# Attention over 16 rows, then a triangle product: reordering the first and last steps of the attention loop

## The chip, the cores and the metric

The kernel runs on one core of a Trainium2 chip. Its five engines each run their own instruction stream and meet at semaphores: TensorE (PE), VectorE (DVE), ScalarE (ACT), GpSimd (POOL) and SyncE (SP), which here only issues DMAs. The metric is the device time of one launch in microseconds (us).

## The reference

Two residual layers on x of shape (16, 32, 32, 32). The change touches the first layer, and the preparation of the second layer's weights and biases. Cut to what matters:

```python
x = x + attention(gn(x))            # layer one, gn: group norm over rows and columns
# attention, for every (a, b) position and 8 heads of 16 channels, over the 16 rows n:
zn = layernorm(z) * ln_w + ln_b
q, k, v = zn @ Wq, zn @ Wk, zn @ Wv
g = sigmoid(zn @ Wg + bg)
att = softmax(einsum('iabhc,jabhc->ijabh', q, k) / 4, axis=1)
out = (einsum('ijabh,jabhc->iabhc', att, v) * g) @ Wo + bo
x = x + triangle(gn(x))             # layer two
# triangle: a, b = sigmoid(zn @ W_g + b_g) * (zn @ W_l + b_l), two pairs of weights
# k = einsum('bitc,bjtc->bijc', a, b); sigmoid(zn @ W_go + b_go) * (norm(k) @ W_lo + b_lo)
```

## The kernel before

Every engine's order is written out by hand; there is no scheduler. The first layer is a software pipeline over eight blocks of four columns b (NS = 8, a block is 128 x 512 values). Period j works on three blocks at once: block j from its layer norm to its score exponentials, block j-1 from the softmax sum to the transposed probabilities ("tail"), block j-2 from the product with z to the gated output and the residual ("B"). Periods 0 to 2 stand in front of a loop of four, written periods 3 to 6; periods 7, 8 (NS) and 9 (NS + 1) stand behind it. Periods 8 and 9 have no block j of their own, and period 9 has no tail.

What one period holds, in the names of the code and of the profile:

- TensorE: `pe_u` (products of the transposed probabilities PT with Z, to `u_sb`), `pe_znT` (transposes of `zn_tok`), `pe_t` (znT with A_bd, eight heads, in three banks, so head h waits for the low part of head h-3), `pe_o` (u_sb with Wv_p), `pe_PT` (four transposes of P), `pe_scores` (t_sb with zbd, four groups), `pe_gate`, `pe_out` (og with Wo_h).
- float32 values go to TensorE as a high and a low float16 part. For t: ACT casts the high part (L628), DVE subtracts the low part (L936). For the probabilities P, which lie in `S_sb` as float32: ACT casts P's high part into `PP` (`p_high`, L622), and `p_low` (L444) subtracts; in period 1 DVE does that, in all later periods POOL. For the normalised block: ACT casts `zn_tok` (`act_ln_high`, L588), POOL subtracts its low part (`pool_ln_low`, L431).
- DVE also takes the scores' maximum (`nmax`, L953) and subtracts it (L957), sums the exponentials (L868) and inverts the sums (`rden`, L887), gates the output (`gate_o`, `og`, L907), copies two of four transposed groups of P (`PT_copy`, L912; ACT has the other two, L644), adds the residual (`dve_x1`, L897) and reduces x1 and its square for the second group norm (`dve_stats`, L873, and `dve_stats_sq`, L879).
- ACT also makes the exponentials (`exps`, L634), the gates' tanh (`gates`, L639) and the copies of u (L614).
- POOL: the layer norm's power (`pool_ln_rstd`, L418), the normalisation of P by `rden` (`pool_norm`, L438), the layer norm's scale and shift (`pool_ln_scale`, L423 to L427), `pool_sqx` (x1 squared, L451), `pool_ln_low`, and the group-normed block j+3 (`pool_ln_front`, L410 to L414).

`dve_weights2` splits the second layer's weights into high and low parts: 28 small instructions on 32 partitions (L977 to L989). `dve_biases2` splits its biases in three: 6 small instructions (L995 to L1004). POOL then spreads the three bias parts into `B1` (L554) and clears two buffers of 128 x 4096 float32 (L549: `x_tok`, L558: `PP`). TensorE takes the first product of the second layer's statistics (`g2_mm`) only when all of that preparation has been counted (`wprep2`), and when DVE has summed the statistics of all eight blocks.

Of the kernel before, what the change touches and what calls it, by code (L numbers as in the profile page):

```python
# [28 lines left out]
NS = L // SB  # L29
# [7 lines left out]
def build(nc, x, ln_w, ln_b, Wq, Wk, Wv, Wg, bg, Wo, bo, al_in, be_in, W_la, b_la, W_ga, b_ga,  # L37
          W_lb, b_lb, W_gb, b_gb, al_o, be_o, W_go, b_go, W_lo, b_lo, out):
    ctx = ExitStack()
    with ctx:  # L40
# [392 lines left out]
        def pool_norm(pool, m, ks):  # L433

            pool.wait_ge(p_rec, 2 * m + ks[0] // 2 + 1)
            for k in ks:
                P = S_sb[:, 8 * k:8 * k + 8].rearrange("p q a n -> p (q a) n")
                nc.gpsimd.tensor_tensor(P, P, bcast(rden[:, 32 * k:32 * k + 32], 2, N), ALU.mult).then_inc(p_nrm, 1)  # L438
# [13 lines left out]

        def pool_period(pool, j, par, tail=True, stats=True):
            LN = j + 1 < NS
            own = tail and not (j == 1)
            if LN:
                pool_ln_rstd(pool, j + 1, 1 - par)
            if tail:
                pool_norm(pool, j - 1, (0, 1))
                pool_norm(pool, j - 1, (2, 3))  # L460
            if LN:
                pool_ln_scale(pool, j + 1, 1 - par)
            if own:
                p_low(pool, nc.gpsimd, j - 1, (0, 1))
            if stats:
                pool_sqx(pool, j - 3)
            if own:
                p_low(pool, nc.gpsimd, j - 1, (2, 3))
            if LN:
                pool_ln_low(pool, j + 1, 1 - par)  # L470
            if j + 3 < NS:
                pool_ln_front(pool, j + 3, 1 - par)
# [134 lines left out]
        def act_period(act, j, par, half, tail=True, B=True, A=True, LN=True):  # L607
# [34 lines left out]
            def PT_copy(k):  # L642
                act.wait_ge(pt_mm, 4 * m + k + 1)
                nc.scalar.copy(PT[:, 8 * k:8 * k + 8].rearrange("p q m -> p (q m)"),  # L644
                               bank_b(k)[:, :].bitcast(f16)).then_inc(pt_ok[1], 1)
# [7 lines left out]
            if early:  # L653

                if j == 0:
                    t_high(range(5))
                    act_ln_square(act, 2, 0)
                    t_high(range(5, H))
                    act_ln_high(act, 1, 1, 0)
                    nc.scalar.activation(scrap[:, 0:1], minus_half[:, 0:1], ACT.Tanh)  # L660
                    act_weights(act)
                else:
                    t_high((0, 1, 2))
                    p_high((0, 1))
                    t_high((3, 4))
                    p_high((2, 3))
                    act_ln_square(act, 3, 1)
                    t_high((5, 6, 7))
                    PT_copy(1)
                exps((0,))  # L670
                gates((0, 1))
                exps((1,))
                if j == 1:
                    PT_copy(3)
                gates((2, 3))
                if j == 0:
                    act_znT(act, 1)
                else:
                    act_ln_high(act, 2, 0, 1)
                exps((2, 3))  # L680
                return
            if A:
# [217 lines left out]
        def dve_period(dve, j, par, tail=True, B=True, A=True, stats=True):  # L900
# [23 lines left out]
                dve_ln_centre(dve, j + 2, par)  # L924
            if stats:
                dve_stats(dve, s - 1)
            if j == NS:
                dve_weights2(dve)
            if j == NS + 1:
                dve_biases2(dve)  # L930

            for h in range(H if A else 0):
                if h == 3 and B:
                    gate_o(range(A2))
                dve.wait_ge(t_hi, H * j + h + 1)
                nc.vector.tensor_tensor(t_sb[:, LO, :, h], bank_tg(h)[:, :].rearrange("p (q i) -> p q i", i=N),  # L936
                                        t_sb[:, HI, :, h], ALU.subtract).then_inc(t_lo, 1)
                if j == 0 and h == 0:
                    dve_gate_weights(dve)
                if j == 0 and h == 2:  # L940
                    dve_ln_centre(dve, 2, 0)
                if j == 1 and h in (2, 4):
                    p_low(dve, nc.vector, 0, (h - 2, h - 1))
            if B and not A:
                gate_o(range(A2))
            if tail:
# [3 lines left out]
            for k in range(4 if A else 0):  # L950
                S = bank_s(k)[:, :].rearrange("p (r n) -> p r n", n=N)
                dve.wait_ge(s_mm, 4 * j + k + 1)
                nc.vector.tensor_reduce(nmax[:, k % 2], S, op=ALU.max, axis=AX.X).then_inc(s_max, 1)  # L953
                if tail:
                    dve.wait_ge(p_lo, 4 * m + k + 1)
                dve.wait_ge(s_max, 4 * j + k + 1)
                nc.vector.tensor_tensor(S_sb[:, 8 * k:8 * k + 8].rearrange("p q a n -> p (q a) n"), S,  # L957
                                        bcast(nmax[:, k % 2], 2, N), ALU.subtract).then_inc(s_sub, 1)
                if k == 1 and stats:
                    dve_stats_sq(dve, s - 1)  # L960
                if k == 2 and tail:
                    PT_copy(2)
            if stats and not A:
                dve_stats_sq(dve, s - 1)
            if tail and not A:
                PT_copy(2)

        WP1 = 3 + 4 + 1 + 1

# [581 lines left out]
```

## Time and profile before

| what | us |
|---|---|
| median of 3 runs (lowest, highest) | 329.82 (329.68, 332.94) |
| the profiled execution: its time | 330.46 |
| its span in the trace | 328.4 |
| busy in the span: PE, DVE, ACT, POOL | 245.6, 256.8, 214.8, 196.9 |
| share of the chain that ended last: DVE, PE, ACT, issue, POOL | 43%, 35%, 7%, 5%, 5% |
| mean granted clock of TensorE (share of full) | 0.907 |

Rows of the timeline have the start, the duration, the engine, the line of kernel.py, the instruction, what it writes and reads, and in brackets the idle time in front of it with the instruction that ended it. A row with x2 to x64 is a run of like instructions. Rows of the chain have start, duration and what stood on the path that ended last.

### The profile page before, as it was taken

Reading aid. Unit: us, or ns where it says so; the run is one execution under the profiler, and the core shown is the slowest. Engines: PE = TensorE matmul, PEld = TensorE weight load, DVE = VectorE, ACT = ScalarE, POOL = GpSimd, SP = SyncE. Lnnn points to the kernel's source line nnn. Section 1 sums busy time; section 2 is a strip of 40 time slices with the busy share of each in tenths; the row PEclk is TensorE's granted clock in tenths of the full one; section 3 lists DMA queues with packets and bytes.
Section 4 is the critical chain, followed back from the end, with each engine's and each line's share of the span. In section 5 each row is a group of like instructions: output and inputs, shape, how many; then the busy total and the mean of one; then the engine's idle time right before and its main releaser. Section 6 shows DMA issues by size and latency. Waiting matters only on the chain.

```text
span 328.4 us, 8118 instructions
## 1 busy us (share of the span) xinstructions
PE 245.6 (75%) x3326; PEld 148.7 (45%) x3326; DVE 256.8 (78%) x451; ACT 214.8 (65%) x393; POOL 196.9 (60%) x172
## 2 busy tenths in 40 slices
PE   0055956688779889889899899792386398999983
PEld 0045523166266366356356455560351134555663
DVE  4985798997779899899897896899767665442683
ACT  4734679469759878788789688693171255775390
POOL 6891686806988988988958827329056367000052
PEclk9995699599969999999999999997589579999996
DMA  7200204002203112113032032200000003655115
GB/s 244 49 0 0 65 26 106 2 2 64 66 2 98 32 43 67 26 54 73 6 83 49 2 85 69 45 2 1 0 2 2 1 0 70 165 155 146 52 57 199
DMA packets 32576, 18.14 MB, mean 55 GB/s; under 512 B 21084, under 2 KB 29596, under 8 KB 32540
## 3 DMA queue, kind: packets, MB, share of 16 engines
q1 hardware_dynamic: 32540, 17.63, 19.9%
q8 instruction: 26, 0.43, 0.6%
q14 instruction: 10, 0.08, 0.1%
HBM read 8.18 MB, written 5.77 MB: 42 GB/s over the span
## 4 chain that ended last, share of the span: by engine, by line
DVE 43%; PE 35%; ACT 7%; issue 5%; POOL 5%; DMA 2%; SPq 1%; DVEq 0%; ACTq 0%
PE PS L1189 30%; DVE t_sb L936 5%; DVE nmax L953 5%; DVE S_sb L957 4%; DVE og L907 4%; DVE gn_part L1019 3%; DVE sums L868 3%; DVE Z L1179 2%; PE PS L1258 2%; DVE PP L912 2%; DVE xT L897 1%; PE PS L1206 1%; DVE W_p L977 1%; DMA x_tok<-in_x 1%; ACT t_sb L628 1%
## 5 line engine op out<-in xcount | busy, mean ns | idle before, releaser
L1189 PE MATMUL PS<-znT,A_bd 128*128 128x512 f16 x192 | 49.5, 404 | 14.9 <-DVE t_sb L936 13.5
L438 POOL TENSOR_TENSOR S_sb<-S_sb,rden 128x512 f32<-128x512 f32 x32 | 35.0, 1117 | 25.7 <-DVE rden L887 25.7
L936 DVE TENSOR_TENSOR t_sb<-PS,t_sb 128x512 f16<-128x512 f32 x64 | 41.0, 685 | 10.0 <-ACT t_sb L628 9.9
L628 ACT CAST t_sb<-PS 128x512 f16<-128x512 f32 x64 | 36.4, 608 | 17.2 <-PE PS L1189 16.1
L1189 PEld LDWEIGHTS PS<-znT,A_bd 128*128 128x128 f16 x192 | 17.5, 102 | 45.4 <-DVE t_sb L936 27.1
L444 POOL TENSOR_TENSOR PP<-S_sb,PP 128x512 f16<-128x512 f32 x28 | 32.0, 1157 | 5.6 <-ACT PP L622 5.6
L1189 PEld LDWEIGHTS PS<-PP,Z 128*128 128x128 f16 x512 | 29.2, 114 | 12.9 <-issue 12.3
L614 ACT COPY u_sb<-PS 128x512 f32<-128x512 f32 x64 | 32.7, 616 | 1.8 <-PE PS L1189 1.8
L1189 PE MATMUL PS<-zbd,t_sb 128*128 128x64 f16 x768 | 27.7, 196 | 6.8 <-DVE t_sb L936 4.5
L1189 PEld LDWEIGHTS PS<-zbd,t_sb 128*128 128x128 f16 x768 | 25.0, 100 | 15.1 <-DVE S_sb L957 6.6
L1189 PE MATMUL PS<-PP,Z 128*128 128x128 f16 x512 | 31.3, 219 | 0.5 <-DVE S_sb L957 0.4
L1258 PE MATMUL PS<-ident,PP 128*128 128x128 f16 x256 | 19.7, 236 | 12.2 <-DVE og L907 10.3
L634 ACT ACTIVATE S_sb<-S_sb 128x512 f32<-128x512 f32 x32 | 20.3, 640 | 12.4 <-DVE S_sb L957 12.4
L644 ACT COPY PP<-PS 128x1024 f16<-128x1024 f16 x16 | 16.2, 1011 | 16.6 <-PE PS L1258 16.6
L957 DVE TENSOR_TENSOR S_sb<-PS,nmax 128x512 f32<-128x512 f32 x32 | 22.2, 692 | 3.1
L1139 DVE SCALAR_TENSOR_TENSOR u_sb<-S_sb,PS 128x128 f32<-128x128 f32 x64 | 14.1, 282 | 13.4 <-ACT S_sb L781 13.3
L1258 PEld LDWEIGHTS PS<-ident,PP 128*128 128x128 f16 x256 | 16.9, 106 | 16.1 <-DVE og L907 11.2
L953 DVE TENSOR_REDUCE nmax<-PS 128x32 f32<-128x512 f32 x32 | 21.9, 683 | 2.1 <-PE PS L1189 2.1
L907 DVE SCALAR_TENSOR_TENSOR og<-th,PS 128x512 f32<-128x512 f32 x32 | 19.9, 682 | 3.2 <-PE PS L1189 3.1
L418 POOL TENSOR_TENSOR ln_rs<-ln_ve,minus_half 128x16 f32<-128x16 f32 x7 | 20.4, 2914 | 2.3 <-DVE ln_ve L864 2.3
L622 ACT CAST PP<-S_sb 128x512 f16<-128x512 f32 x32 | 18.9, 661 | 2.8 <-POOL S_sb L438 2.7
L639 ACT ACTIVATE th<-PS,bg_h 128x512 f32<-128x512 f32 x32 | 20.3, 691 | 0.0
(206 smaller groups left out, 541.6 us busy)
## 6 DMA issues: line engine op xcount, KB each, us to landing
Z<-zn_dram SPq DMA_DIRECT2D x64, 64.0 KB, 2.9
x_tok<-in_x SPq DMA_DIRECT2D x4, 512.0 KB, 5.8
zn_dram<-zn_tok SPq DMA_DIRECT2D x8, 256.0 KB, 2.0
zbd<-znT SPq DMA_DIRECT2D x32, 64.0 KB, 2.0
out_x<-u_sb SPq DMA_DIRECT2D x4, 512.0 KB, 3.2
k_dram<-og SPq DMA_DIRECT2D x3, 512.0 KB, 4.8
th<-k_dram SPq DMA_DIRECT2D x12, 128.0 KB, 2.8
PP<-u_sb SPq DMA_DIRECT2D x8, 128.0 KB, 2.6
```

The source lines that it names most:

```text
L418: nc.gpsimd.tensor_tensor(ln_rs[:, par], ln_ve[:, par], minus_half[:, 0:A2 * SB], ALU.pow).then_inc(ln_z, 1)
L438: nc.gpsimd.tensor_tensor(P, P, bcast(rden[:, 32 * k:32 * k + 32], 2, N), ALU.mult).then_inc(p_nrm, 1)
L444: ops.tensor_tensor(P2[:, 8 * k:8 * k + 8, LO], P, P2[:, 8 * k:8 * k + 8, HI], ALU.subtract).then_inc(p_lo, 1)
L614: nc.scalar.copy(u_sb[:, :, 4 * k:4 * k + 4].rearrange("p h q i -> p q h i"), bank_u(k)[:, :].rearrange("p (q h i) -> p q h i", q=4, h=H)) ...
L628: nc.scalar.copy(t_sb[:, HI, :, h], bank_tg(h)[:, :].rearrange("p (q i) -> p q i", i=N)).then_inc(t_hi, 1)
L634: nc.scalar.activation(v, v, ACT.Exp).then_inc(s_exp, 1)
L907: nc.vector.scalar_tensor_tensor(out=og[:, k], in0=th[:, par, k], scalar=1.0, in1=bank_o(k)[:, :], op0=ALU.add, op1=ALU.mult).then_inc(o_o ...
L936: nc.vector.tensor_tensor(t_sb[:, LO, :, h], bank_tg(h)[:, :].rearrange("p (q i) -> p q i", i=N), t_sb[:, HI, :, h], ALU.subtract).then_in ...
L953: nc.vector.tensor_reduce(nmax[:, k % 2], S, op=ALU.max, axis=AX.X).then_inc(s_max, 1)
L957: nc.vector.tensor_tensor(S_sb[:, 8 * k:8 * k + 8].rearrange("p q a n -> p (q a) n"), S, bcast(nmax[:, k % 2], 2, N), ALU.subtract).then_i ...
L1189: return nc.tensor.matmul(o, l, r, start=start, stop=stop)
L1258: last = nc.tensor.transpose(bank_b(k)[:, :].bitcast(f16)[:, 128 * (q % 8):128 * (q % 8) + 128], P2[:, q].rearrange("p k m -> p (k m)"), i ...
```

## The change

Four moves; no arithmetic changes.

- Period 1: the four low parts of block 0's P go from DVE to POOL, between `pool_norm` of block 0 and `pool_ln_scale` of block 2.
- Period 1: ACT's cast of block 2's `zn_tok` (L588 in the kernel before, `act_ln_high(act, 2, 0, 1)`) goes from behind the gates to ahead of the first exponential.
- Periods 8 and 9: `dve_weights2` goes from ahead of period 8's gating to the end of period 8, and `dve_biases2` from period 9 to stand right behind it. DVE's third P copy comes ahead of the reduction of x1 squared.
- Period 8: POOL's `sqx` comes behind all four low parts of P.

```diff
--- before.py
+++ after.py
@@ -452,20 +452,23 @@
 
         def pool_period(pool, j, par, tail=True, stats=True):
             LN = j + 1 < NS
-            own = tail and not (j == 1)
             if LN:
                 pool_ln_rstd(pool, j + 1, 1 - par)
             if tail:
                 pool_norm(pool, j - 1, (0, 1))
                 pool_norm(pool, j - 1, (2, 3))
+            if j == 1:
+                p_low(pool, nc.gpsimd, j - 1, range(4))
             if LN:
                 pool_ln_scale(pool, j + 1, 1 - par)
-            if own:
+            if tail and j > 1:
                 p_low(pool, nc.gpsimd, j - 1, (0, 1))
-            if stats:
+            if stats and j < NS:
                 pool_sqx(pool, j - 3)
-            if own:
+            if tail and j > 1:
                 p_low(pool, nc.gpsimd, j - 1, (2, 3))
+            if stats and j >= NS:
+                pool_sqx(pool, j - 3)
             if LN:
                 pool_ln_low(pool, j + 1, 1 - par)
             if j + 3 < NS:
@@ -667,6 +670,7 @@
                     act_ln_square(act, 3, 1)
                     t_high((5, 6, 7))
                     PT_copy(1)
+                    act_ln_high(act, 2, 0, 1)
                 exps((0,))
                 gates((0, 1))
                 exps((1,))
@@ -675,8 +679,6 @@
                 gates((2, 3))
                 if j == 0:
                     act_znT(act, 1)
-                else:
-                    act_ln_high(act, 2, 0, 1)
                 exps((2, 3))
                 return
             if A:
@@ -924,10 +926,6 @@
                 dve_ln_centre(dve, j + 2, par)
             if stats:
                 dve_stats(dve, s - 1)
-            if j == NS:
-                dve_weights2(dve)
-            if j == NS + 1:
-                dve_biases2(dve)
 
             for h in range(H if A else 0):
                 if h == 3 and B:
@@ -939,8 +937,6 @@
                     dve_gate_weights(dve)
                 if j == 0 and h == 2:
                     dve_ln_centre(dve, 2, 0)
-                if j == 1 and h in (2, 4):
-                    p_low(dve, nc.vector, 0, (h - 2, h - 1))
             if B and not A:
                 gate_o(range(A2))
             if tail:
@@ -960,10 +956,13 @@
                     dve_stats_sq(dve, s - 1)
                 if k == 2 and tail:
                     PT_copy(2)
+            if tail and not A:
+                PT_copy(2)
             if stats and not A:
                 dve_stats_sq(dve, s - 1)
-            if tail and not A:
-                PT_copy(2)
+            if j == NS:
+                dve_weights2(dve)
+                dve_biases2(dve)
 
         WP1 = 3 + 4 + 1 + 1
 
```

ScalarE, period 1, from the last high parts of t to the end of the period (th: gates, S_sb: exponentials, PP<-PS: the P copies). Before:

```order
L628 CAST t_sb<-PS 128x32x16 x3
L644 COPY PP<-PS 128x1024
L634 ACTIVATE S_sb<-S_sb 128x512
L639 ACTIVATE th<-PS,bg_h 128x512 x2
L634 ACTIVATE S_sb<-S_sb 128x512
L644 COPY PP<-PS 128x1024
L639 ACTIVATE th<-PS,bg_h 128x512 x2
L588 CAST zn_tok<-zc 128x512
L634 ACTIVATE S_sb<-S_sb 128x512 x2
```

and now:

```order
L631 CAST t_sb<-PS 128x32x16 x3
L647 COPY PP<-PS 128x1024
L591 CAST zn_tok<-zc 128x512
L637 ACTIVATE S_sb<-S_sb 128x512
L642 ACTIVATE th<-PS,bg_h 128x512 x2
L637 ACTIVATE S_sb<-S_sb 128x512
L647 COPY PP<-PS 128x1024
L642 ACTIVATE th<-PS,bg_h 128x512 x2
L637 ACTIVATE S_sb<-S_sb 128x512 x2
```

The cast of zn_tok now stands ahead of the first exponential; before, it stood behind all gates, ahead of the last two exponentials.

GpSimd, period 1 and the head of period 2, from the normalisation of block 0's P. Before:

```order
L438 TENSOR_TENSOR S_sb<-S_sb,rden 128x512 x4
L423 TENSOR_TENSOR zc<-zc,ln_rs 128x512
L425 TENSOR_TENSOR zc<-zc,w_bc 128x512
L427 TENSOR_TENSOR zc<-zc,b_bc 128x512
L431 TENSOR_TENSOR zn_tok<-zc,zn_tok 128x512
L410 TENSOR_TENSOR zc<-x_tok,gn_r 128x512
L414 TENSOR_TENSOR zc<-zc,gn_sh 128x512
L418 TENSOR_TENSOR ln_rs<-ln_ve,minus_half 128x16
L438 TENSOR_TENSOR S_sb<-S_sb,rden 128x512 x4
```

and now:

```order
L438 TENSOR_TENSOR S_sb<-S_sb,rden 128x512 x4
L444 TENSOR_TENSOR PP<-S_sb,PP 128x8x64 x4
L423 TENSOR_TENSOR zc<-zc,ln_rs 128x512
L425 TENSOR_TENSOR zc<-zc,w_bc 128x512
L427 TENSOR_TENSOR zc<-zc,b_bc 128x512
L431 TENSOR_TENSOR zn_tok<-zc,zn_tok 128x512
L410 TENSOR_TENSOR zc<-x_tok,gn_r 128x512
L414 TENSOR_TENSOR zc<-zc,gn_sh 128x512
L418 TENSOR_TENSOR ln_rs<-ln_ve,minus_half 128x16
```

The four low parts (PP) stand in front of the three instructions that scale block 2.

VectorE, periods 8 and 9. Before, from the last of the weights' instructions (W_p, Wgo_bd) to the residual of period 9 (xT):

```order
L985 TENSOR_TENSOR W_p<-w_f,W_p 32x64 x2
L989 TENSOR_TENSOR Wgo_bd<-w_f,Wgo_bd 32x32
L985 TENSOR_TENSOR W_p<-w_f,W_p 32x64 x2
L989 TENSOR_TENSOR Wgo_bd<-w_f,Wgo_bd 32x32
L907 SCALAR_TENSOR_TENSOR og<-th,PS 128x512 x4
L912 COPY PP<-PS 128x1024
L879 TENSOR_REDUCE st<-sqx 128x16
L912 COPY PP<-PS 128x1024
L897 SCALAR_TENSOR_TENSOR xT<-PS,bo_col,xT 128x512
```

and now, from the reduction of x1 (st<-xT) to the first of the weights' instructions:

```order
L875 TENSOR_REDUCE st<-xT 128x16
L909 SCALAR_TENSOR_TENSOR og<-th,PS 128x512 x4
L914 COPY PP<-PS 128x1024 x2
L881 TENSOR_REDUCE st<-sqx 128x16
L976 CAST W_p<-w_f 32x64 x2
```

Before, the 28 instructions for the weights stood between that reduction and og; now og and both P copies follow the reduction directly, then the reduction of sqx, and the weights begin behind it.

## Rows read from the trace of the kernel before

**Rows 1.** The chain that ended last, periods 1 and 2: start, us, what

```profile
75.13 1.01 ACT zn_tok L588
...
83.26 4.08 POOL S_sb L438 x4
...
91.03 1.12 POOL PP L444
```

**Rows 2.** Timeline of POOL, periods 1 and 2

```profile
60.47 1.04 POOL L423 TENSOR_TENSOR zc<-zc,ln_rs 128x512 f32<-128x512 f32 x1
...
76.20 1.45 POOL L431 TENSOR_TENSOR zn_tok<-zc,zn_tok 128x512 f16<-128x512 f32 x1 [11.35 <-ACT zn_tok L588]
```

**Rows 3.** Timeline of ACT, periods 1 and 2

```profile
63.51 1.14 ACT L622 CAST PP<-S_sb 128x512 f16<-128x512 f32 x2
...
66.63 0.58 ACT L628 CAST t_sb<-PS 128x512 f16<-128x512 f32 x1 [0.16 <-PE PS L1189]
...
70.76 0.63 ACT L634 ACTIVATE S_sb<-S_sb 128x512 f32<-128x512 f32 x1 [2.22 <-DVE S_sb L957]
...
87.41 1.54 ACT L628 CAST t_sb<-PS 128x512 f16<-128x512 f32 x3
```

**Rows 4.** Timeline of DVE, periods 1 and 2

```profile
61.31 2.42 DVE L444 TENSOR_TENSOR PP<-S_sb,PP 128x512 f16<-128x512 f32 x2
...
69.16 0.17 DVE L864 TENSOR_SCALAR ln_ve<-ln_var 128x16 f32<-128x16 f32 x1
...
78.47 0.55 DVE L887 RECIPROCAL rden<-sums 128x64 f32<-128x64 f32 x1
...
84.47 2.48 DVE L907 SCALAR_TENSOR_TENSOR og<-th,PS 128x512 f32<-128x512 f32 x4
...
95.66 0.69 DVE L953 TENSOR_REDUCE nmax<-PS 128x32 f32<-128x512 f32 x1 [0.15 <-PE PS L1189]
```

**Rows 5.** The chain that ended last, periods 3 and 4 of the loop

```profile
104.80 0.61 PE PS L1206 x8
...
112.01 1.88 DVE og L907 x3
...
118.76 0.60 DVE nmax L953
...
127.95 0.61 PE PS L1206 x8
```

**Rows 6.** Timeline of DVE, periods 8 and 9

```profile
221.91 1.75 DVE L977 CAST W_p<-w_f 32x64 f16<-32x64 f32 x2
...
229.20 0.30 DVE L977 CAST W_p<-w_f 32x64 f16<-32x64 f32 x2
...
232.15 2.48 DVE L907 SCALAR_TENSOR_TENSOR og<-th,PS 128x512 f32<-128x512 f32 x4
...
237.65 0.69 DVE L912 COPY PP<-PS 128x1024 f16<-128x1024 f16 x1 [0.60 <-PE PS L1258]
...
242.15 3.99 DVE L995 TENSOR_SCALAR b_in<-b_in 128x64 f32<-128x64 f32 x1
...
247.75 2.48 DVE L907 SCALAR_TENSOR_TENSOR og<-th,PS 128x512 f32<-128x512 f32 x4 [0.18 <-PE PS L1189]
```

**Rows 7.** Timeline of POOL, periods 8 and 9

```profile
226.78 2.27 POOL L444 TENSOR_TENSOR PP<-S_sb,PP 128x512 f16<-128x512 f32 x2
...
242.57 3.52 POOL L549 MEMSET x_tok<- 128x4096 f32 x1
```

**Rows 8.** Timeline of PE, period 8

```profile
222.07 2.35 PE L1189 MATMUL PS<-u_sb,Wv_p 32*32 32x512 f32 x64 [1.02 <-ACT u_sb L614]
234.69 2.92 PE L1258 MATMUL PS<-ident,PP 128*128 128x128 f16 x24 [10.27 <-DVE og L907]
```

**Rows 9.** Stretches of 2 us: length, PE busy, granted clock, DMA share, GB/s

```profile
92.00:94.00 2.00, 1.70 (x15) 0.50 0.00 0
...
226.00:228.00 2.00, 0.00 (x0) 0.58 0.00 0
```

## The prediction

> **What bounds the kernel now.** I read four views. First the chain that ended last: in the loop it alternates between TensorE and VectorE, and each period takes 127.95 - 104.80 = 23.15 us [rows 5]. It leaves that pattern at two places, which are the loop's ends. Around period 2 it runs over GpSimd for 16 us without a break: from ScalarE's cast of zn_tok at 75.13 over GpSimd's work to the low part of P at 91.03, for which TensorE's transposes wait [rows 1]. In period 8 it sits in VectorE's weight instructions. Then the timelines of GpSimd, ScalarE and VectorE around period 2, for who is early and who is late [rows 2 to 4]; the same for period 8 [rows 6 to 8]; last the granted clock in stretches of 2 us [rows 9]. The reader is to see two things. GpSimd had scaled block 2 long before its cast came: it stood idle for 11.35 us, until 76.20 [rows 2]. And TensorE stood idle for 10.27 us in period 8, until og came from VectorE [rows 8], which had its input since 224.42 and began at 232.15 [rows 6, 8].
>
> **Period 1, the low parts off VectorE.** Four instructions leave VectorE; the first two took 2.42 us together [rows 4], so some 3.7 us of VectorE's time. I expect almost none of it at the end of the t stage. The last heads' low parts need ScalarE's high parts, and ScalarE itself waited for TensorE there: its last cast began at 66.63 and ended at 67.21 [rows 3]. One low part of 0.6 us behind it ends at 67.8, where VectorE's last one ended at about 67.9 before. Gain here 0.1. What the move costs is on GpSimd: low parts 0 and 1 from 60.47, where the scaling used to start [rows 2], at 1.13 each [2.27 for two, rows 7]: until 62.8. Parts 2 and 3 need ScalarE's casts that begin at 63.51 (0.57 each) [rows 3]: 64.15 to 66.45. The scaling takes 91.03 - 87.34 = 3.69 [rows 1], so zn_tok's input is ready at 70.15 instead of about 64.9.
>
> **Period 1, the cast ahead.** ScalarE had been idle for 2.22 us before its first exponential at 70.76, and was busy nearly without a gap from there [rows 3]. With the cast first, 70.2 to 71.25, the first exponential is 0.5 late and the last ones, which no longer have the cast ahead of them, some 0.5 early. So 5.0 us of the wait for the cast go: GpSimd's low part of zn_tok begins at 71.3 instead of 76.20, and everything that stood behind it without a gap, the front of block 4, the power and the normalisation, moves 4.9 forward: the normalisation of block 1's P from 83.26 [rows 1] to 78.4. The reciprocals that it needs end at 79.0 [rows 4], for its second pair only, which would start at 80.5. The store of zn_tok, and behind it the loads of Z for block 1 on SP's queue, go forward with it; nobody waited for them.
>
> **What is late next.** ScalarE's casts of P no longer wait. Its casts of the heads 3 and up began at 87.41 [rows 3] and now can at about 85. Then TensorE and VectorE set the pace, as in the loop. There, from the second og (112.01) to the first maximum (118.76) it takes 6.75 [rows 5], from the first og 0.62 more: 7.37. The first og of period 2 began at 84.47 [rows 4]. With the 0.5 of ScalarE's lead it would be 83.9. I doubt that lead: VectorE's small instruction at 69.16 took 0.17 with GpSimd idle [rows 4], and now falls in GpSimd's scaling. It belongs to the kind that waits for GpSimd (below), for up to one GpSimd instruction, 1.28 at most, and the scores' chain behind it would slip by as much as ScalarE gained. So I take 84.47: the maximum at 91.84 instead of 95.66 [rows 4], 3.8 earlier. From there to the next transposes of zn_tok the loop takes 127.95 - 118.76 = 9.19 with one reduction that period 2 has not (0.6), so 8.6; before it took 104.80 - 95.66 = 9.14 [rows 4, 5], at half clock for its first part [rows 9]. That gives 0.5 more. **Sum of period 1's edits: 4.4 us**, with ends 3.0 (half of the front lost again) and 5.4 (VectorE isn't held, and the lead counts).
>
> A rule speaks against this edit. A low part takes GpSimd 1.13 [rows 7], and VectorE 0.6 to 0.7 where it isn't held up (of the 2.42 for two one part is a hold-up [rows 4]). The Trainium skill (GPSIMD Engine Reference, Engine selection) puts elementwise work with two inputs on VectorE, since GpSimd takes about twice as long: the trace agrees on the ratio. By that rule alone the four parts would cost 4 x 0.5 = 2 us; by the rows it is GpSimd's idle time that pays.
>
> **Period 8, og first.** TensorE's o products end at 222.07 + 2.35 = 224.42, and VectorE is free from about 222 [rows 6, 8]. og then starts at 224.44 instead of 232.15: **7.7 us**. P's low parts must keep up. TensorE's transposes start at og's end, 226.9; GpSimd's low parts 0 and 1 are done at 225.8, and the last two, now ahead of sqx, at 228.1 instead of 229.05 [rows 7]. The four groups are needed one after another from 226.9 on, so that none is late in either order: this reordering is worth nothing, nor is that of the third P copy, which waited for TensorE at 237.65 [rows 6] with the reduction already done.
>
> **Period 8, the weights behind.** Price before: from 221.91 to 232.15, 10.2 us for 28 instructions. The first eight took 7.3 us, until 229.20, the other twenty 2.95 [rows 6], and GpSimd's last low part ended at 229.05 [rows 7]. The dear eight stand exactly where GpSimd is busy. Likewise the biases' first instruction took 3.99 us [rows 6] beside GpSimd's clearing of x_tok, which ended at 246.09 [rows 7]; the five others took 1.43 in all. In the new place GpSimd has finished sqx (229.1), and its next work waits for x1, which stands on VectorE behind the biases. So I price them undisturbed: 28 x 0.148 = 4.1, and 0.2 + 1.4 = 1.6 for the biases. Place: the third copy ends at 237.65 + 0.69 - 7.7 = 230.6, the reduction at 231.2, the weights at 235.3, the biases at 236.9, the residual and its reduction at 238.2. Period 9's og needs TensorE at 247.75 - 7.7 = 240.0 [rows 6]: 1.8 us of cover, so they cost nothing. If they took their old 10.2 and 5.4, they would end at 246.8, the two others at 248.1, and all of the 7.7 would be gone. The clearing of x_tok moves too, to 238 to 242, then the spreading of the biases to 244, then the other clearing to 247.5; the second layer's first product would come near 247.4 and needs only the spreading. This is near enough to name, and costs nothing by these times.
>
> Such holding of one engine by the other is seen above. The Trainium skill (SBUF — State Buffer, Who interferes with whom) says that VectorE's copies, casts and tensor-scalars can lock a port pair that GpSimd shares, whole instructions long. The trace agrees: 0.87 against 0.15 us for the same cast. By that rule the old place was dear and the new one isn't, as the rows have it already.
>
> **Sum.** 330.46 - 4.4 - 7.7 = 318.4 for the profiled execution; the median of the runs lies 0.64 below it, so 317.7.
>
> **The rivals.** (1) ScalarE, blocked by its own cast: if GpSimd is held in its low parts or its scaling (one part took some 1.7 on VectorE [rows 4]), the cast comes 1 to 2 us later, all exponentials stand behind it, and period 1's edits are worth 2 to 3 instead of 4.4. 319.1 to 320.1. For it: the cast has no slack against 70.76. (2) A better clock: TensorE's clock fell from 2.4 to 1.2 GHz within 226 to 228, in its idle stretch [rows 9]. With og first the stretch is 2.5 us instead of 10.3. If the clock stays up, the transposes lose less (24 of them took 2.92 at half clock [rows 8], of which some 1.3 would go), and if VectorE isn't held at 69.16 either, the time is 315.8. Against it: a mean of 0.58 over 226 to 228 puts the fall near 226.3, before og can end. (3) The weights are slow by themselves, not through GpSimd: the time is 329.8 - 4.4 + 0.3 = 325.7; with nothing from period 1 either (the cast's front all lost on ScalarE) it is 330, no change. Against it: twenty cheap instructions in a row once GpSimd had ended. (4) Slower: the loop settles into another phase, in which TensorE has an idle stretch in every period and the clock falls, as in period 2 [rows 9]. There it stayed at half, 1.2 GHz, for some three such stretches; each holds up to 1.70 us of work, of which half is lost, together some 2.1 where the chain runs over TensorE. From six periods on this is more than the 12.1 won; in seven (2 to 8) it costs 14.7, and the time is 332.3. Against it: periods 3 to 6 are set by TensorE and VectorE themselves [rows 5], which both only move.
>
> **How the numbers follow.** Forecast 0.57; rival 1 0.14; rival 2 0.18; rival 3 with period 1's gain 0.06, and with no gain 0.03; rival 4 0.02. The forecast's own range is 316.5 to 319.2. The range from 315.3 to 321.0 holds rivals 1 and 2 as well, with some room for where the second layer meets the clock's falls. A change under 1% (3.3 us) is about what can't be told from none. Faster by more: 0.95; within: 0.03; slower: 0.02.
>
> **What would show it.** In period 1: GpSimd's idle before the low part of zn_tok falls from 11.35 to about 1; the first exponential starts 0.5 late; the normalisation of block 1 starts near 78.5; the first maximum of period 2 near 91.8; the zn_tok transposes of period 3 near 100.4. Periods 3 to 7 keep their lengths. In period 8: TensorE's idle before the transposes 2.5; 28 weight instructions in about 4 us with no gap before period 9's og. Wrong would be: casts of the weights near 0.9 us each, a wait of ScalarE for GpSimd past 71, or a low part of P that TensorE waits for in either place.

## The result, and the profile after

| | before | changed |
|---|---|---|
| median, us | 329.75 (329.53 to 332.94, 4 runs) | 315.77 (315.18 to 317.63, 4 runs) |
| ratio to before | | 0.9593, 95% interval 0.9555 to 0.9631 |
| profiled execution, us; its span | 330.46; 328.4 | 315.18; 313.0 |
| mean granted clock | 0.907 | 0.951 |

The change makes the kernel 14.0 us faster. The forecast was 317.7 us, 12.1 faster.

To see where the 15.4 us between the two traces are, I cut both spans at five marks that every version has: S, the start of the second sum of exponentials of period 1 (all edits come later); Z, period 3's transposes of zn_tok; the first og of periods 8 and 9; and zc, the first normalised values of the second layer (VectorE's TENSOR_SCALAR, L477 before, L480 now).

| stretch, us | before | changed | difference |
|---|---|---|---|
| start to S | 55.80 | 54.79 | -1.01 |
| S to Z | 49.00 | 44.18 | -4.82 |
| Z to og of period 8 | 127.35 | 119.60 | -7.75 |
| og of period 8 to og of period 9 | 15.60 | 15.25 | -0.35 |
| og of period 9 to zc | 11.79 | 11.54 | -0.25 |
| zc to the end | 68.86 | 67.64 | -1.22 |

The second and third rows are the two ends of the loop, where the edits are. The first can't be the change's, as nothing ahead of S differs.

The chain that ended last, changed kernel, periods 1 and 2. The stretch over GpSimd of [rows 1] is gone. A shorter one is new ahead of the cast: from 63.20 the chain runs over GpSimd's last two low parts and its scaling. From ScalarE's cast on it runs over the exponentials, the copies of u, TensorE and VectorE:

```profile
63.20 2.27 POOL PP L444 x2
...
69.20 1.09 ACT zn_tok L591
70.29 0.53 ACT S_sb L637
...
75.60 1.93 ACT u_sb L617 x4
...
78.50 4.40 PE PS L1188 x71
...
83.49 1.88 DVE og L909 x3
...
98.97 0.61 PE PS L1205 x8
```

GpSimd's timeline, changed kernel, periods 1 and 2: the idle time in front of the low part of zn_tok is 1.20 instead of 11.35 [rows 2], and the normalisation begins at 77.36, 22.57 after S instead of 27.46 [rows 1]. One idle time of 1.48 is new, for ScalarE's third cast of P:

```profile
63.20 2.27 POOL L444 TENSOR_TENSOR PP<-S_sb,PP 128x512 f16<-128x512 f32 x2 [1.48 <-ACT PP L625]
...
70.37 1.44 POOL L431 TENSOR_TENSOR zn_tok<-zc,zn_tok 128x512 f16<-128x512 f32 x1 [1.20 <-ACT zn_tok L591]
...
77.36 4.56 POOL L438 TENSOR_TENSOR S_sb<-S_sb,rden 128x512 f32<-128x512 f32 x4
```

ScalarE's, same stretch: the cast waits for GpSimd, and the first exponential follows it without a gap, 15.40 after S instead of 14.96 [rows 3]:

```profile
69.20 1.09 ACT L591 CAST zn_tok<-zc 128x512 f16<-128x512 f32 x1 [2.18 <-POOL zc L427]
70.19 0.63 ACT L637 ACTIVATE S_sb<-S_sb 128x512 f32<-128x512 f32 x1
```

VectorE's, same stretch: the time freed of low parts has turned into waits for ScalarE's casts. The small instruction at 67.79 took 0.17, og begins 28.10 after S (28.67 before), the first maximum 35.36 after S (39.86 before) [rows 4]:

```profile
62.64 0.69 DVE L934 TENSOR_TENSOR t_sb<-PS,t_sb 128x512 f16<-128x512 f32 x1 [0.59 <-ACT t_sb L631]
64.68 1.89 DVE L934 TENSOR_TENSOR t_sb<-PS,t_sb 128x512 f16<-128x512 f32 x3 [1.35 <-ACT t_sb L631]
...
67.79 0.17 DVE L866 TENSOR_SCALAR ln_ve<-ln_var 128x16 f32<-128x16 f32 x1
...
82.89 2.48 DVE L909 SCALAR_TENSOR_TENSOR og<-th,PS 128x512 f32<-128x512 f32 x4
...
90.15 0.69 DVE L949 TENSOR_REDUCE nmax<-PS 128x32 f32<-128x512 f32 x1
```

Period 8, VectorE's timeline, changed kernel. og waits for TensorE now; the weights' 28 instructions run from 225.21 to 229.15, 3.94 instead of 10.24, and the biases' first one takes 0.20 instead of 3.99 [rows 6]. In front of period 9's og VectorE idles 1.52:

```profile
218.57 2.48 DVE L909 SCALAR_TENSOR_TENSOR og<-th,PS 128x512 f32<-128x512 f32 x4 [2.40 <-PE PS L1188]
...
225.21 0.29 DVE L976 CAST W_p<-w_f 32x64 f16<-32x64 f32 x2
...
229.15 0.20 DVE L994 TENSOR_SCALAR b_in<-b_in 128x64 f32<-128x64 f32 x1
...
230.82 0.75 DVE L899 SCALAR_TENSOR_TENSOR xT<-PS,bo_col,xT 128x512 f32<-128x512 f32 x1
...
233.82 2.48 DVE L909 SCALAR_TENSOR_TENSOR og<-th,PS 128x512 f32<-128x512 f32 x4 [1.52 <-PE PS L1188]
```

TensorE's timeline there, and the granted clock: 2.53 of idle time instead of 10.27 [rows 8]. The profile puts the wait down to GpSimd's low parts, but og ended within 0.1 us of the third of them, and in ends_no_reorder (below) the same wait of 2.53 is put down to og:

```profile
221.11 2.87 PE L1257 MATMUL PS<-ident,PP 128*128 128x128 f16 x24 [2.53 <-POOL PP L444]
```

```profile
220.00:222.00 2.00, 0.89 (x10) 0.80 0.00 0
222.00:224.00 2.00, 1.95 (x17) 0.50 0.00 0
224.00:226.00 2.00, 1.87 (x16) 0.85 0.04 8
```

### The profile page after: what moved, and what is told of

It is laid out like the page before. It is cut to its first block, busy times and chain, and to the rows that moved or that the text cites. A ratio compares the mean times of both kernels' runs of the same rounds, so it can differ in the third digit from the quotient of the medians.

```text
span 313.0 us, 8114 instructions
## 1 busy us (share of the span) xinstructions
PE 239.4 (76%) x3321; PEld 145.3 (46%) x3326; DVE 242.9 (78%) x447; ACT 214.4 (68%) x393; POOL 200.7 (64%) x176
## 4 chain that ended last, share of the span: by engine, by line
DVE 40%; PE 36%; ACT 9%; issue 5%; POOL 4%; DMA 2%; SPq 1%; DVEq 0%; ACTq 0%
PE PS L1188 32%; DVE t_sb L934 5%; DVE nmax L949 5%; DVE S_sb L953 4%; DVE og L909 4%; DVE gn_part L1018 4%; DVE sums L870 3%; DVE Z L1178 2%; ACT u_sb L617 2%; POOL PP L444 2%; DVE PP L914 2%; ACT t_sb L631 2%; DVE xT L899 2%; PE PS L1205 1%; DMA x_tok<-in_x 1%
## 5 line engine op out<-in xcount | busy, mean ns | idle before, releaser
L1188 PE MATMUL PS<-znT,A_bd 128*128 128x512 f16 x192 | 48.6, 399 | 14.1 <-DVE t_sb L934 12.5
L444 POOL TENSOR_TENSOR PP<-S_sb,PP 128x512 f16<-128x512 f32 x32 | 36.5, 1156 | 7.0 <-ACT PP L625 7.0
L1188 PE MATMUL PS<-zbd,t_sb 128*128 128x64 f16 x768 | 26.6, 193 | 7.8 <-DVE t_sb L934 5.0
L1188 PEld LDWEIGHTS PS<-zbd,t_sb 128*128 128x128 f16 x768 | 23.8, 98 | 16.3 <-DVE S_sb L953 7.1
L1257 PE MATMUL PS<-ident,PP 128*128 128x128 f16 x256 | 18.6, 229 | 2.7 <-POOL PP L444 2.5
L1188 PE MATMUL PS<-u_sb,Wv_p 32*32 32x512 f32 x512 | 18.8, 598 | 2.0 <-ACT u_sb L617 2.0
```

Of the source, the lines that this page charges most:

```text
L444: ops.tensor_tensor(P2[:, 8 * k:8 * k + 8, LO], P, P2[:, 8 * k:8 * k + 8, HI], ALU.subtract).then_inc(p_lo, 1)
L1188: return nc.tensor.matmul(o, l, r, start=start, stop=stop)
```

## The experiments

Twelve kernels, in three groups. Each was run and timed next to the kernel before on one chip. The medians of before were 329.14, 329.39 and 328.97 us in the three groups, so I compare ratios; the changed kernel's is 0.9593. Each table below has the stretches from one profiled execution each.

**Group 1: the parts alone.**

p1_only undoes the weights' move and the two reorderings, p8_weights_only does nothing else than the move. Diffs against the kernel before:

```diff
 # p8_weights_only
-            if j == NS:
-                dve_weights2(dve)
-            if j == NS + 1:
-                dve_biases2(dve)
...
+            if j == NS:
+                dve_weights2(dve)
+                dve_biases2(dve)
```

```diff
 # cast_only (p1_only has this and low_only)
                     PT_copy(1)
+                    act_ln_high(act, 2, 0, 1)
                 exps((0,))
...
-                else:
-                    act_ln_high(act, 2, 0, 1)
```

```diff
 # low_only
+            if j == 1:
+                p_low(pool, nc.gpsimd, j - 1, range(4))
             if LN:
                 pool_ln_scale(pool, j + 1, 1 - par)
...
-                if j == 1 and h in (2, 4):
-                    p_low(dve, nc.vector, 0, (h - 2, h - 1))
```

Expected of p1_only: 

> Both edits of period 1 alone; the weights, biases, sqx and the third P copy stay where they were. Theory A (the two ends are independent, and the shift of 4.8 us that the trace after shows between period 1 and period 3 stays to the end): 4.6 to 5.2 us faster than before, 324.6 to 325.2. Theory B (part of that shift is only there with the other end changed, or is lost in the clock of the second layer): under 3.5 us faster. Period 3's zn_tok transposes should start about 4.8 earlier against the sums of period 1 than before.

Expected of p8_weights_only: 

> Only the weights and biases moved behind period 8's gating and P copies; period 1, sqx and the order of the third P copy as before. Theory A (7.7 us from og's start, some 1 us more from TensorE's clock falling later and returning sooner): 8.0 to 9.2 us faster, 320.6 to 321.8, and the weights' 28 instructions take about 4 us. Theory B (the order of sqx and of the copy is needed as well): at least 1 us less than that, with TensorE waiting for a low part of P in period 8. Theory C (the weights are dear by themselves): no gain.

Expected of cast_only: 

> Only ScalarE's cast of zn_tok goes ahead of the first exponential; the low parts of block 0 stay on VectorE. Theory A (the cast's place is the whole gain of period 1, and the low parts' move is worth nothing): 4.5 to 5.5 us faster, 324.3 to 325.3; GpSimd's scaling is then done before the cast's turn, so that the cast starts near 68.5 and the first exponential is not late. Theory B (the low parts on VectorE hold the t stage and with it everything behind): 2 to 3.5 us faster only.

Expected of low_only: 

> Only the low parts of block 0 go to GpSimd; the cast of zn_tok stays behind the gates. Theory A (VectorE's freed 3.7 us turn into waits for ScalarE's casts, GpSimd's idle time pays): 0 to 0.4 us faster, 329.4 to 329.8; the last low part of t ends at most 0.3 earlier. Theory B (VectorE is the bound of the t stage): 1.5 to 3.7 us faster.

| | median, us | ratio, 95% interval | S to Z | Z to og 8 | og 8 to og 9 |
|---|---|---|---|---|---|
| p1_only | 324.45 | 0.9846, 0.9802 to 0.9889 | 44.23 | 127.01 | 15.29 |
| p8_weights_only | 319.49 | 0.9702, 0.9668 to 0.9736 | 48.88 | 119.61 | 14.28 |
| cast_only | 322.96 | 0.9813, 0.9745 to 0.9880 | 43.93 | 126.78 | 15.62 |
| low_only | 329.47 | 1.0005, 0.9977 to 1.0033 | 48.72 | 126.80 | 15.60 |

The ends are independent as far as the intervals tell: 1.54% and 2.98% make 4.5%, the whole change 4.1%. p1_only won 4.7 us, as its theory A said. p8_weights_only won 9.65 us at the median, 0.45 above what was expected; its og stretch is 1.0 shorter than the changed kernel's (see the clock, below). cast_only won 6.2 by its median, 0.7 above what was expected, but its four runs lie 4 us apart; its trace has 5.07 in the stretch S to Z. The low parts' move is worth nothing that can be seen, and the cast's place is all of period 1. In cast_only ScalarE takes the cast as soon as its own queue allows, and still waits 1.23 for the first exponential:

```profile
68.51 1.10 ACT L588 CAST zn_tok<-zc 128x512 f16<-128x512 f32 x1
70.84 0.63 ACT L634 ACTIVATE S_sb<-S_sb 128x512 f32<-128x512 f32 x1 [1.23 <-DVE S_sb L956]
```

```profile
69.69 1.42 POOL L431 TENSOR_TENSOR zn_tok<-zc,zn_tok 128x512 f16<-128x512 f32 x1 [4.81 <-ACT zn_tok L588]
```

and in low_only GpSimd's idle time only shrinks by what it now does itself, from 11.35 [rows 2] to 5.71 and a new 1.48, while VectorE waits for ScalarE's casts of t, as in the changed kernel (up to 1.35):

```profile
74.77 1.44 POOL L431 TENSOR_TENSOR zn_tok<-zc,zn_tok 128x512 f16<-128x512 f32 x1 [5.71 <-ACT zn_tok L590]
```

**Group 2: the cover in period 8, and why the weights were dear.**

ends_no_reorder has everything but the orders of sqx and of the third P copy. Diffs of the other three against the changed kernel:

```diff
 # gpsimd_beside, behind pool_sqx of period 8; t_sb is free there
+            if j == NS:
+                pool.wait_ge(p_lo, 4 * NS)
+                for i in range(8):
+                    E = S_sb[:, 0:8].rearrange("p q a n -> p (q a n)")
+                    F = t_sb[:, :].rearrange("p k q h i -> p (k q h i)").bitcast(f32)[:, 512 * i:512 * i + 512]
+                    nc.gpsimd.tensor_tensor(F, E, E, ALU.mult)
```

```diff
 # biases_back
             if j == NS:
                 dve_weights2(dve)
-                dve_biases2(dve)
...
                 dve_stats(dve, s - 1)
+            if j == NS + 1:
+                dve_biases2(dve)
```

```diff
 # weights_twice, in dve_weights2; sq is free there
             for g in range(A2):
+                rows = slice(D * g, D * g + D)
+                for i in range(5):
+                    nc.vector.tensor_copy(sq[rows, 64 * i:64 * i + 64], w12_f[rows, 64:128])
+                for i in range(2):
+                    nc.vector.tensor_copy(sq[rows, 512 + 32 * i:544 + 32 * i], w12_f[rows, 128:160])
```

Expected of ends_no_reorder: 

> The changed kernel without its two small reorderings in period 8 (GpSimd's sqx behind the low parts, VectorE's third P copy ahead of the reduction). Theory A (they are worth nothing, as nobody waits for either): 13.4 to 14.9 us faster than before, the same as the whole change within 1 us, and TensorE waits for no low part of P. Theory B (the transposes of period 8, which the trace after puts behind GpSimd's third low part, are held up by sqx ahead of it): 1 us less gain.

Expected of gpsimd_beside: 

> The changed kernel with eight extra GpSimd products of 128 x 512 float32 behind sqx in period 8, some 9 us of work beside VectorE's weights, into memory that nobody reads. Theory A (a GpSimd instruction holds the next cast or copy of VectorE until it ends): some six of the weights' instructions take about 1.1 us instead of 0.15, period 9's og starts 4 to 5.5 later, and the kernel is only 8.5 to 10 us faster than before. Theory B (the weights were dear ahead of og for another reason): no cast over 0.3 us and 13.4 to 14.9 us faster.

Expected of biases_back: 

> The changed kernel with the biases where they were, ahead of period 9's og, beside GpSimd's clearing of x_tok. Theory A (the clearing holds their first instruction until it ends, and what covered it before, TensorE's work up to period 9's og, ends 1.5 to 2 us too early now that x1 comes sooner): the first instruction takes about 3.5 to 4 us, og of period 9 starts some 2 later, 11.4 to 13 us faster than before. Theory B (the biases were hidden there anyway and still are): 13.4 to 14.9 us faster.

Expected of weights_twice: 

> The changed kernel with 28 extra casts and copies of the weights' size ahead of the weights, into a scratch buffer. They add 28 times 0.148 = 4.1 us of VectorE's work. Theory A (the cover is the 1.5 us of idle time ahead of period 9's og): og starts 2.6 later, and the kernel is 11 to 12.3 us faster than before. Theory B (there is no cover, every microsecond counts): 9.5 to 10.5 us faster. Theory C (VectorE is not the bound up to period 9's og, by much): 13.4 to 14.9 us faster.

| | median, us | ratio, 95% interval | S to Z | og 8 to og 9 | zc to end |
|---|---|---|---|---|---|
| changed (above) | 315.77 | 0.9593, 0.9555 to 0.9631 | 44.18 | 15.25 | 67.64 |
| ends_no_reorder | 315.35 | 0.9584, 0.9539 to 0.9629 | 43.91 | 14.29 | 67.80 |
| gpsimd_beside | 321.70 | 0.9765, 0.9701 to 0.9828 | 43.93 | 18.80 | 70.35 |
| biases_back | 319.26 | 0.9690, 0.9649 to 0.9730 | 44.74 | 17.06 | 68.18 |
| weights_twice | 317.90 | 0.9649, 0.9613 to 0.9684 | 44.18 | 16.41 | 67.65 |

The two reorderings are worth nothing that can be seen. gpsimd_beside settles why the weights were dear: same place, same instructions, but GpSimd is busy for 8.04 us beside them. VectorE's timeline, then GpSimd's:

```profile
226.13 1.83 DVE L982 CAST W_p<-w_f 32x64 f16<-32x64 f32 x2
227.88 1.06 DVE L984 CAST Wgo_bd<-w_f 32x32 f16<-32x32 f32 x1
228.86 1.08 DVE L985 COPY Wlo_bd<-w_f 32x32 f32<-32x32 f32 x1
...
232.86 0.16 DVE L985 COPY Wlo_bd<-w_f 32x32 f32<-32x32 f32 x1
...
239.05 2.47 DVE L915 SCALAR_TENSOR_TENSOR og<-th,PS 128x512 f32<-128x512 f32 x4
```

```profile
224.86 8.04 POOL L477 TENSOR_TENSOR t_sb<-S_sb 128x512 f32<-128x512 f32 x8
```

The casts and copies take 0.9 to 1.1 until 232.90, where GpSimd ends, and 0.15 to 0.18 from there. The weights take 9.87 us in all instead of 3.94, and og of period 9 comes 3.55 late and shows no wait. 4 to 5.5 were expected there; the weights began 0.76 sooner behind og than in the changed kernel, since TensorE's clock didn't fall in this execution (below). The kernel lost 5.9 us, more than the 4 to 5.5 expected. 2.7 of them lie behind zc in the trace, where its work is the same. Lined up at zc, the traces show two steps there. The first is 0.75 us near 8 us behind zc: TensorE's clock stood at half for 8.6 us behind zc, and for 6.6 in the changed kernel. The second is 1.9 us near 20 us behind it: the 64 products with `u_sb` ran at half clock. Here they are in the changed kernel and in gpsimd_beside:

```profile
263.07 1.96 PE L1188 MATMUL PS<-PP,u_sb 128*32 128x128 f32 x64 [1.55 <-DMA PP<-u_sb]
```

```profile
269.63 3.62 PE L1194 MATMUL PS<-PP,u_sb 128*32 128x128 f32 x64 [1.88 <-DMA PP<-u_sb]
```

Whether the extra work or this one execution made the clock fall there is not shown. In biases_back one instruction waits for the whole clearing:

```profile
231.61 3.98 DVE L995 TENSOR_SCALAR b_in<-b_in 128x64 f32<-128x64 f32 x1
...
237.06 2.48 DVE L909 SCALAR_TENSOR_TENSOR og<-th,PS 128x512 f32<-128x512 f32 x4
```

```profile
232.03 3.51 POOL L552 MEMSET x_tok<- 128x4096 f32 x1
```

It costs 1.8 at period 9's og, and 3.2 to 3.5 in the whole, more than the 1 to 2.6 expected. Of the rest, 0.56 is in the stretch S to Z, which has the same instructions as the changed kernel: there VectorE's small instruction ahead of the maxima was held by GpSimd in this execution, for 1.02 instead of 0.17, and everything behind it came 0.57 later:

```profile
69.05 1.02 DVE L866 TENSOR_SCALAR ln_ve<-ln_var 128x16 f32<-128x16 f32 x1
```

What hid the biases in the kernel before was TensorE's work up to period 9's og. There they began 10.00 us behind period 8's og, and the o products ended 15.56 behind it, with 0.2 to spare. In biases_back the weights have taken the same room: the biases begin 11.61 behind og, and the o products end 15.05 behind it. weights_twice added 3.14 us of VectorE's work (4.1 estimated; its plain copies were cheaper), and og came 1.16 later instead of the 2.6 expected: 1.5 of the 3.14 was covered, and 0.4 came from a third P copy that was a little earlier. The kernel was 11.5 us faster than before, within what theory A said. Counted from S, its trace is 1.18 longer than the changed kernel's; the medians are 1.8 to 2.1 apart, and the rest is not explained.

**Group 3: what bounds the changed kernel, and a better one.** Diffs against it:

```diff
 # p_high_early
+                    p_high((2, 3))
                     t_high((3, 4))
-                    p_high((2, 3))
```

```diff
 # og_banks_first
             if B and not A:
-                gate_o(range(A2))
+                gate_o((2, 3, 0, 1) if j == NS else range(A2))
...
             if ks[0] == 0 and s >= 1:
-                pe.wait_ge(o_ok, HP * s)
+                pe.wait_ge(o_ok, HP * s - (2 if s == NS - 1 else 0))
...
-                pe.wait_ge(o_ok, HP * s + k + 1)
+                pe.wait_ge(o_ok, HP * (s + 1) if s == NS - 2 else HP * s + k + 1)
```

```diff
 # filler: n matmuls of znT into bank 7
             if not B:
-                pe_t(pe, j)
+                pe_t(pe, j, (0, 1, 2))
+                if j == 1:
+                    filler(16)
+                pe_t(pe, j, range(3, H))
...
                 pe_o(pe, s)
                 if m < NS:
+                    pe.wait_ge(x1_ok, NS - 2)
+                    filler(9)
```

all_three has all of these, with filler(4) in period 8.

Expected of p_high_early: 

> The changed kernel with ScalarE's casts 2 and 3 of block 0's P ahead of its fourth and fifth cast of t in period 1, where it stood idle for 3 us. Theory A (the changed kernel's chain in period 1 runs from TensorE's slow t matmuls over these casts to GpSimd): GpSimd's last two low parts start about 1.5 earlier, the cast of zn_tok near 1.5 earlier, and the kernel is 0.3 to 0.8 us faster than the changed one (14.3 to 14.8 faster than before), since VectorE's scores hold the rest. Theory B (TensorE and VectorE alone set period 1): the same as the changed kernel.

Expected of og_banks_first: 

> The changed kernel with period 8's four gatings in the order 2, 3, 0, 1, so that the two banks into which TensorE transposes P are free after two of them. Theory A (og is the wait that ends last in period 8): the transposes start 1.25 earlier, ahead of the fall of TensorE's clock, and period 9's og comes 1.5 to 2.3 earlier: 15.5 to 16.5 us faster than before. Theory B (GpSimd's low parts of P are the bound there by now): 14 to 14.6 faster.

Expected of filler: 

> The changed kernel with matmuls of no use in TensorE's two idle stretches: 16 of 512 columns in period 1 behind the third head, 9 in period 8 ahead of the transposes, into a bank that nobody reads. Theory A (the clock at half right behind these stretches costs time on the chain): the granted clock stays at 1 in both places, period 3's transposes come 1.0 to 1.5 earlier and period 9's og 0.8 to 1.3 earlier on top: 15.5 to 16.8 us faster than before. Theory B (the slow matmuls are hidden behind VectorE's and ScalarE's work): 13.7 to 14.6 faster.

Expected of all_three: 

> The changed kernel with all three: the early casts of P, the banks' order in period 8, and filler matmuls (16 in period 1, 4 in period 8). If each holds and they add where they don't overlap: 16.5 to 18.5 us faster than before. If VectorE's own work is the floor in both places: 15 to 16.

| | median, us | ratio, 95% interval | S to Z | og 8 to og 9 | zc to end |
|---|---|---|---|---|---|
| p_high_early | 315.81 | 0.9599, 0.9569 to 0.9628 | 43.22 | 15.14 | 67.30 |
| og_banks_first | 314.50 | 0.9563, 0.9530 to 0.9595 | 44.09 | 13.22 | 68.06 |
| filler | 315.48 | 0.9591, 0.9561 to 0.9621 | 42.93 | 14.33 | 68.24 |
| all_three | 313.90 | 0.9547, 0.9513 to 0.9580 | 42.71 | 13.15 | 71.27 |

Each edit does in the trace what it was made for, as far as one trace each can say. p_high_early takes the wait out of GpSimd's low parts, and ScalarE's third cast of P starts 3.28 after S instead of 7.71. But the small VectorE instruction between the t stage and the maxima is now held by GpSimd, 0.78 instead of 0.17:

```profile
60.08 0.62 ACT L625 CAST PP<-S_sb 128x512 f16<-128x512 f32 x1 [0.40 <-POOL S_sb L438]
...
69.70 1.07 ACT L591 CAST zn_tok<-zc 128x512 f16<-128x512 f32 x1 [1.41 <-POOL zc L427]
```

```profile
68.92 0.78 DVE L866 TENSOR_SCALAR ln_ve<-ln_var 128x16 f32<-128x16 f32 x1
```

og_banks_first starts the transposes 1.4 us after the o products, when both the second og and GpSimd's second low part had just ended (both near 220.6), with the clock at full (1.00 from 216 to 224). The next two groups then wait for a copy that stands behind all four og:

```profile
220.63 1.07 PE L1257 MATMUL PS<-ident,PP 128*128 128x128 f16 x16 [1.42 <-POOL PP L444]
222.51 1.05 PE L1257 MATMUL PS<-ident,PP 128*128 128x128 f16 x16 [0.82 <-DVE PP L914]
```

filler keeps the clock at full in both places (here the window in period 1 that stood at 0.50 in the changed kernel), and the stretches are 1.25 and 0.92 shorter:

```profile
60.00:62.00 2.00, 1.48 (x7) 1.00 0.00 0
62.00:64.00 2.00, 1.89 (x9) 1.00 0.00 0
```

Two readings of these stretches need care. Seven kernels have the changed kernel's period 1, and their S to Z ranges from 43.91 to 44.74; the 43.22 and 42.93 lie 0.7 and 1.0 below that, about as much as it spans. And og 8 to og 9 took 14.3 in ends_no_reorder without any filler, because the clock didn't fall there, so that filler's 14.33 is what a kernel has when the clock stays up, and of og_banks_first's 2.03 about half may be the same.

The medians hold less still: by the ratios, of 329, p_high_early and filler come within 0.2 us of the changed kernel, og_banks_first 1.0 us lower and all_three 1.5 us lower. No hopeful theory came true in the time. p_high_early, og_banks_first (14.5 faster) and all_three (15.1 faster) came out as the less hopeful theory of each said, filler (13.5 faster) just under it. Only all_three's interval lies below the changed kernel's 0.9593, and it overlaps that kernel's own; it has the lowest median of the kernels run.

The stretch from zc to the end has the same instructions in all of these and took 67.3 to 71.3 in their profiled executions. The 71.27 of all_three, whose profiled execution (316.18) was the slowest of its six, can be read from the trace. Lined up at zc, it is 0.6 us ahead of the changed kernel at 33 us behind zc. Then TensorE waits for the DMA that copies `u_sb` into `PP`, which cost no wait in the changed kernel, and its 64 products run partly at half clock; by 45 us behind zc it is 3.6 us late. Changed kernel, then all_three:

```profile
277.07 1.95 PE L1188 MATMUL PS<-PP,u_sb 128*32 128x128 f32 x64
```

```profile
275.88 2.87 PE L1188 MATMUL PS<-PP,u_sb 128*32 128x128 f32 x64 [1.95 <-DMA PP<-u_sb]
```

filler has 1.06 us of the same wait. Whether an earlier first layer brings such waits on or they only vary is not shown: there is one trace per kernel.

## Why the prediction was right, step by step

**Low parts off VectorE, 0.1 forecast.** low_only: 0.28 in S to Z, less than the stretch differs among kernels with the same instructions in it (up to 0.8), and no change in the time. The reason given holds: VectorE waits for ScalarE's casts, which wait for TensorE at half clock.

**The cast ahead.** Forecast: GpSimd's low part at 71.3, 4.9 earlier; measured 70.37, or 71.38 with the 1.01 that this execution was ahead at S. The first exponential was 0.44 late, as 0.5 was said. The sum of 4.4 measured 4.82. The first maximum came 4.50 earlier against 3.8 forecast, and the way from there to period 3's transposes gave 0.32 against 0.5. The 4.50 has a single doubt in it that didn't come true here: the small instruction wasn't held by GpSimd, as it fell into the gap of 0.08 us between two of its instructions (it started at 67.79; GpSimd's second scaling instruction ended at 67.83 and its third began at 67.91). og then had ScalarE's lead, at 83.90 in the old trace's time, which is the better case named, 83.9. This is luck. biases_back has the same instructions in period 1; there the small one took 1.02, og began 28.67 after S, which is the 84.47 that the prediction took, and S to Z was 44.74. It is one of seven kernels with this period 1; in the other six, the changed kernel among them, the small instruction took 0.17 or 0.18.

**What pays for the low parts.** GpSimd's idle time, as said. It follows from cast_only that nothing had to be paid: with the low parts left on VectorE, period 1's whole gain is there. The prediction costed the pair and never asked what the cast does without the move.

**og first, 7.7.** 7.75. **The reorderings, nothing.** Nothing, in ends_no_reorder. **The weights at 4.1 and 1.6.** 3.94 and 1.64, and the cover of 1.8 was 1.52. That GpSimd was the cause is shown by gpsimd_beside, which undoes rival 3. The prediction named as a sign of being wrong a low part of P that TensorE waits for. The profile shows one in period 8, but og ended with it, and ends_no_reorder has the same wait behind og. The clearing of PP ended at 241.71, and the second layer's first small VectorE copy began at 241.67 and took 0.17: near, as said, and without cost.

**The rest: 1.9 us of the medians not forecast.** The 315.77 is inside the range given, but below the forecast's own, 316.5 to 319.2. It is beside rival 2's 315.8, and that too is luck. Rival 2 asked for two things: that VectorE isn't held, which was so, and that the clock stays up, which wasn't. The clock fell near 221.2 and was back near 224.6; before it had been at half from 226.3 to 240.0. The stretch up to period 9's og took 0.35 less. In p8_weights_only, ends_no_reorder and gpsimd_beside it didn't fall there at all, and in the first two the stretch is 14.3 instead of 15.25. The reorderings aren't the reason, since gpsimd_beside has both. So rival 2's price for the clock was about right, 1.0 to 1.3 (14.3 against 15.25 and 15.60), and with one trace each it isn't shown what decides whether it is paid. Its clock row is this one, of ends_no_reorder:

```profile
220.00:222.00 2.00, 0.30 (x6) 1.00 0.00 0
222.00:224.00 2.00, 1.41 (x23) 1.00 0.00 0
```

Another 0.25 and 1.22 lie from period 9's og to the end, where no edit reaches and where the forecast put nothing. Nearly all of the 1.22 goes with TensorE's clock. 0.44 comes 8 us behind zc, where the clock was at half until 7.8 us behind zc before and until 6.6 now. 0.7 comes at the very end, where the last twelve transposes of the output ran partly at half clock before (1.67 and 1.06 us) and at full now (1.16 and 0.66). Other versions took 67.3 to 71.3 for this stretch, so whether the change brought this about or it is chance is open. Rival 1 (ScalarE blocked) didn't happen: GpSimd's low parts took 1.13 each. Rival 4 didn't: the loop's period stayed at 23.15 (98.97 to 122.12 in the changed kernel). Its 332.3 should read 332.4, which changes nothing.

## What to carry to other kernels

Look at a pipeline's first and last periods by themselves: one cast on ScalarE moved ahead of work that needn't wait for it won 1.9% (1.2 to 2.6%), and small preparation moved behind the gating that TensorE waits for won 3.0%. Before small copies are moved on VectorE, look at what GpSimd does beside them at both places, since the price of the same copy differed sevenfold (1.19 and 0.16 us). Idle time that hides a cost can be spent only once: the weights moved into the room that had hidden the biases, which had to move as well. And when a gain of 1 us is looked for, compare the stretch that was edited with the same stretch in kernels that don't touch it, since it can move by as much through a small instruction's luck or the clock.

## What the runs showed of the hardware that I had not expected

A GpSimd clearing of 128 x 4096, which reads nothing, held a VectorE tensor-scalar of 64 values in each partition: with the end of sqx ahead of it, for 3.98 to 4.00 us in each of the five kernels that had the biases there. The same clearing ran beside four og of the changed kernel, which took 0.62 each as elsewhere.

TensorE's clock fell behind an idle stretch of the same length in some kernels and not in others. Seven kernels had 2.5 us of idle time in front of period 8's transposes. In four of them (the changed kernel, p_high_early, biases_back, weights_twice) it fell to 1.2 GHz 2.4 to 3.8 us behind og's start. In ends_no_reorder, p8_weights_only and gpsimd_beside it stayed at 2.4 GHz up to period 9's og.

A VectorE instruction that takes 0.17 us took 0.78 to 1.02 in three kernels (p_high_early, all_three, biases_back), where it began in the middle of one of GpSimd's back-to-back products, and 0.17 in those where it began within 0.05 us of the gap between two of them.

The time to S, ahead of every edit, ranged from 54.62 to 56.80 us over the fourteen profiled executions. Differences of 1 us in this kernel's span can be that alone.
